# Two slots instead of four in a gather table's rows, and whole-set loads with three buffers in the last stage of a four-layer network

## The reference, cut to what matters

```
layer 0: y = leaky(bn(conv1x1(x)));  xp = inproj(y)
         t = leaky(bn(depthwise3x3(y)));  offset, mask = linear(t), softmax(linear(t))
         for each pixel, 4 groups of 64 channels, 9 points:
             bilinear sample of xp at pixel + dilated tap + offset   (4 corners), times mask, summed
         outproj, bn, squeeze-excite, two-layer MLP, residual
layer 1: grouped 3x3 convolution with kernels rotated by a predicted angle, modulated
layer 2: linear attention (8 heads of 64), 1x1 output, batch norm over all 4 images
layer 3: channels 0-63 kept; 64-127 an 11x1, 128-191 a 1x11, 192-255 a 3x3 grouped
         convolution with weights rounded to 4 bits
```

## Time and profile before

| | us |
|---|---|
| median of 3 runs | 7485.81 (7482.09 to 7492.41) |
| the profiled execution: time | 7487.15 |
| the profiled execution: span | 7485.3 |
| POOL busy | 4751.4 (63%) |
| DVE busy | 5173.2 (69%) |
| PE busy | 3828.6 (51%) |
| ACT busy | 1072.8 (14%) |
| chain that ended last: POOL, its issue gaps, PE | 49%, 22%, 13% |

### The profile page before, as it was taken

How to read it: one execution, slowest core, us unless ns; L and a number is a source line. 1 busy time by engine, 2 the same in 40 slices (tenths; PEclk the granted TensorE clock), 3 DMA queues, 4 the chain that set the end, 5 groups by cost and what they waited for, 6 DMA issues and landing times.

```text
span 7485.3 us, 45646 instructions
## 1 busy us (share of the span) xinstructions
PE 3828.6 (51%) x10560; PEld 2011.8 (27%) x10560; DVE 5173.2 (69%) x5212; ACT 1072.8 (14%) x1619; POOL 4751.4 (63%) x4676
## 2 busy tenths in 40 slices
PE   5243142351475526632764346426656652589957
PEld 3121021220232214411322124213223431234523
DVE  3778778786777768866777679767777975432545
ACT  1110100000111002211110022101001210121333
POOL 0577777777777777777777777777777777200000
PEclk9666576675687767866887678768878876799978
DMA  6373563754433333355333333553333355201067
GB/s 167 109 206 98 178 183 99 220 149 138 148 122 124 101 103 116 123 203 173 122 123 113 103 111 123 191 181 128 122 113 105 122 175 178 79 34 36 34 177 166
DMA packets 681090, 991.26 MB, mean 132 GB/s; under 512 B 413984, under 2 KB 483616, under 8 KB 665248
## 3 DMA queue, kind: packets, MB, share of 16 engines
q0 software_dynamic: 221184, 604.27, 25.2%
q1 hardware_dynamic: 459808, 385.87, 17.2%
HBM read 792.21 MB, written 197.59 MB: 132 GB/s over the span
## 4 chain that ended last, share of the span: by engine, by line
POOL 49%; issue 22%; PE 13%; DVE 9%; DMA 4%; SPq 2%; ACT 1%; DVEq 0%; POOLq 0%; ACTq 0%
POOL ring L369 48%; PE PS L690 12%; DVE ring L1337 3%; DVE dbuf L1343 2%; DMA img<-d_dram 2%; DMA ring<-table,idx_stage 1%; SPq L483 1%; ACT img L1059 1%; DMA cb<-o_dram 1%; DVE sm L1749 0%; DMA o_dram<-img 0%; POOL idx_stage L385 0%; DMA d_dram<-dbuf 0%; SPq L618 0%; SPq L639 0%
## 5 line engine op out<-in xcount | busy, mean ns | idle before, releaser
L369 POOL DMA_INDIRECT ring<-table,idx_stage x4608 | 4720.1, 1024 | 1435.2 <-issue 1370.1
L1343 DVE TENSOR_REDUCE dbuf<-ring 128x64 f32<-128x2304 f32 x512 | 2070.1, 4043 | 45.9 <-DMA d_dram<-dbuf 18.4
L1337 DVE TENSOR_TENSOR ring<-ring,wt 128x576 f32<-128x576 f32 x2048 | 1414.0, 752 | 973.7 <-DMA ring<-table,idx_stage 855.1
L690 PE MATMUL PS<-img,wb_sb 128*128 128x512 f32 (+1 forms) x3328 | 1646.8, 656 | 468.9 <-DVE img L1402 296.4
L690 PE MATMUL PS<-img,wa_sb 128*128 (+1 forms) x1984 | 931.4, 631 | 666.5 <-DVE img L1723 248.3
L690 PEld LDWEIGHTS PS<-img,wb_sb 128*128 128x128 f32 x3328 | 694.9, 213 | 1387.0 <-issue 1098.4
L690 PEld LDWEIGHTS PS<-img,wa_sb 128*128 128x128 f32 x1984 | 398.4, 203 | 1170.1 <-issue 1079.3
L690 PE MATMUL PS<-sm,params 128*128 128x4 f32 (+1 forms) x32 | 9.1, 355 | 863.1 <-DVE sm L1381 762.0
L690 PE MATMUL PS<-wa_sb,cb 128*128 128x108 f32 (+1 forms) x1024 | 238.8, 399 | 371.8 <-DVE cb L1402 371.8
L787 PE MATMUL PS<-params,img 128*128 128x128 f32 x256 | 62.9, 427 | 689.1 <-DMA img<-d_dram 689.1
L1059 ACT ACTIVATE img<-PS,sm 128x512 f32<-128x512 f32 x384 | 247.5, 680 | 1092.9 <-PE PS L690 1092.9
(11 more groups left out here) (191 smaller groups left out, 2977.5 us busy)
## 6 DMA issues: line engine op xcount, KB each, us to landing
ring<-table,idx_stage POOLq DMA_INDIRECT x4608, 2.9
table<-cb SPq DMA_DIRECT2D x128, 512.0 KB, 7.3
img<-y_dram SPq DMA_DIRECT2D x64, 512.0 KB, 6.6
q_dram<-img SPq DMA_DIRECT2D x32, 1024.0 KB, 4.3
img<-q_dram SPq DMA_DIRECT2D x32, 1024.0 KB, 6.9
img<-in_x SPq DMA_DIRECT2D x8, 2048.0 KB, 12.2
y_dram<-cb SPq DMA_DIRECT2D x64, 256.0 KB, 3.0
d_dram<-dbuf SPq DMA_DIRECT2D x128, 128.0 KB
```

What stands on the lines that cost most here:

```text
L369: nc.gpsimd.indirect_dma_start(out=ring[:, g, p * CORNERS * GC:(p + 1) * CORNERS * GC], out_offset=None, in_=tab[b], in_offset=bass.Indire ...
L690: return nc.tensor.matmul(o, l, r, start=start, stop=stop, **kw)
L1337: last = vec.tensor_tensor(rg, rg, weights.unsqueeze(2).to_broadcast([P, n, GC]), ALU.mult)
L1343: vec.tensor_reduce(dbuf[:, j, g * GC:(g + 1) * GC], ring[:, g, :].rearrange("p (k c) -> p c k", c=GC), AX_X, ALU.add).then_inc(sem("ring_ ...
```

## The change

- A table row has two slots, the pixel and the pixel one image row below, 512 B. The groups lie one behind the other (`(g r)`), so that the next row is the pixel to the right, and one gather reads two rows, 1 KB. `xp` is stored twice instead of four times; index and weight order follow.
- The zero rows at the start are 16 transfers from 32 partitions, 32 KB each, instead of 16 from 64 partitions, 256 KB each.
- o and x2 lie in DRAM by set: a set is 128 contiguous rows of 8 KB. L3 loads it in one transfer; L2b stores each chunk's o and x2 in two halves of 64 partitions each.
- o has a third buffer, in `idx`. Sets 0 to 2 of the first image are loaded ahead of L2b of the last image; in L3 `load_o(0, (3,))` stands ahead of `load_x(1)`, and later sets are issued one to three sets earlier.

```diff
-TAB_FRONT = W + 1
-TAB_ROWS = HW + P
+TAB_ROWS = W + HW
+TAB_STORES = 2
+OBUFS = 3
-        tab = [dram(f"table{b}", [G * TAB_ROWS, CORNERS * GC]) for b in range(B)]
+        tab = [dram(f"table{b}", [G * TAB_ROWS, 2 * GC]) for b in range(B)]
-        o_dram = dram("o_dram", [B, P, KC, 2, HALFP])
-        x2_dram = dram("x2_dram", [B, P, KC, 2, HALFP])
+        o_dram = dram("o_dram", [B, SETS, P, HALFP])
+        x2_dram = dram("x2_dram", [B, SETS, P, HALFP])
-        obuf = [cb[:, j * HALFP:(j + 1) * HALFP] for j in range(2)]
+        obuf = [cb[:, j * HALFP:(j + 1) * HALFP] for j in range(2)] \
+            + [idx[:].rearrange("p j n -> p (j n)")[:, 0:HALFP].bitcast(F32)]
...
-                    pieces = [(t, first) for t in tab for first in (0, P // 2, HW, HW + P // 2)]
+                    pieces = [(t, first, slot) for t in tab for slot in range(2) for first in (slot * HW, slot * HW + W // 2)]
...
-                        for j, back in enumerate((0, 1, W, W + 1)):
-                            first = c * (CHUNK * G) + (TAB_FRONT - back) * G
-                            sp.dma_start(tab[b][bass.ds(first, CHUNK * G), :].rearrange("(p q) c -> p q c", q=SUBS * G)
-                                         [:, :, j * GC:(j + 1) * GC], src).then_inc(sem(f"t_stored{h}"), 16)
+                        rows_at = tab[b].rearrange("(g r) c -> r g c", g=G)
+                        for slot in range(2):
+                            sp.dma_start(rows_at[bass.ds(c * CHUNK + (1 - slot) * W, CHUNK)][:, :, slot * GC:(slot + 1) * GC]
+                                         .rearrange("(p s) g c -> p s g c", s=SUBS),
+                                         xpt[h].rearrange("p (s g c) -> p s g c", s=SUBS, g=G)).then_inc(sem(f"t_stored{h}"), 16)
...
                         for store, src in ((x2_dram, i2[6 + h]), (o_dram, i2[4 + h])):
-                            sp.dma_start(store[b].rearrange("p k two n -> p (k two) n")
-                                         [:, :, bass.ds(c * (CHUNK // 2), CHUNK // 2)],
-                                         src.rearrange("p (a n) -> p a n", a=KC * 2)).then_inc(sem(f"o_stored{h}"), 16)
+                            for j in range(2):
+                                sets = store[b].rearrange("(j k) (two c) n -> j c (k two) n", j=2, two=2)[j]
+                                sp.dma_start(sets[:, :, bass.ds(c * (CHUNK // 2), CHUNK // 2)],
+                                             src[j * SC:(j + 1) * SC, :].rearrange("p (a n) -> p a n", a=KC * 2))\
+                                    .then_inc(sem(f"o_stored{h}"), 16)
...
-                    load_o(0, (0, 1))
+                    load_o(0, (0, 1, 2))
...
+            def set_of(store, b, q):
+                return store[b][q % 2 * KC + q // 2]
...
             def load_x(b, sets=range(SETS)):
                 for q in sets:
-                    for par in range(2):
-                        sp.dma_start(x3[b % 2][par * SC:(par + 1) * SC, q * HALFP:(q + 1) * HALFP], rows_of(x2_dram, b, q, par))\
-                            .then_inc(sem(f"e_x{b % 2}{q}"), 16)
+                    sp.dma_start(x3[b % 2][:, q * HALFP:(q + 1) * HALFP], set_of(x2_dram, b, q)).then_inc(sem(f"e_x{b % 2}{q}"), 16)
...
-                    if b * SETS + q >= 2:
-                        sp.wait_ge(sem("eA"), b * SETS + q - 1)
-                    for par in range(2):
-                        sp.dma_start(obuf[q % 2][par * SC:(par + 1) * SC], rows_of(o_dram, b, q, par))\
-                            .then_inc(sem(f"e_o{q % 2}"), 16)
+                    m = b * SETS + q
+                    if m >= OBUFS:
+                        sp.wait_ge(sem("eA"), m - OBUFS + 1)
+                    sp.dma_start(obuf[m % OBUFS], set_of(o_dram, b, q)).then_inc(sem(f"e_o{m % OBUFS}"), 16)
...
+                load_o(0, (3,))
                 load_x(1)
-                load_o(0, (2, 3))
-                if B > 1:
-                    load_o(1, (0, 1))
+                load_o(1, (0, 1, 2))
...
-                        if b + 1 < B and form < 2:
-                            load_o(b + 1, (form + 2,))
+                        if form == 0 and b + 1 < B:
+                            load_o(b + 1, (3,))
+                        if form and b + 2 < B:
+                            load_o(b + 2, (form - 1,))
...
                         if form == 0 and b + 2 < B:
-                            load_o(b + 2, (0, 1))
+                            load_o(b + 2, (2,))
```

More of the change, by code:

```diff
@@ L460, in A @@
                     sp.wait_ge(sem("zeros"), 1)
-                    pieces = [(t, first) for t in tab for first in (0, P // 2, HW, HW + P // 2)]
-                    for (t, first), name in zip(pieces, store_sems + ["pads_stored"] * (len(pieces) - len(store_sems))):
-                        sp.dma_start(t.rearrange("(r g) c -> r g c", g=G)[first:first + P // 2],
-                                     dbuf[0:P // 2, 0, :].unsqueeze(1).to_broadcast([P // 2, G, C])).then_inc(sem(name), 16)
+                    pieces = [(t, first, slot) for t in tab for slot in range(2) for first in (slot * HW, slot * HW + W // 2)]
+                    for (t, first, slot), name in zip(pieces, store_sems + ["pads_stored"] * (len(pieces) - len(store_sems))):
+                        sp.dma_start(t.rearrange("(g r) (s c) -> s r g c", g=G, s=2)[slot][first:first + W // 2],
+                                     dbuf[0:W // 2, 0, 0:GC].unsqueeze(1).to_broadcast([W // 2, G, GC])).then_inc(sem(name), 16)
                     for name in store_sems:
@@ L1251, in lb @@
                         done(act, "bP", n)
-                        act.wait_ge(sem(f"o_stored{h}"), m_ * 32 + 16)
+                        act.wait_ge(sem(f"o_stored{h}"), m_ * 64 + 16)
                         room(act, "bS", n)
@@ L1271, in scaled @@
                     for q in range(SETS):
-                        act.wait_ge(sem(f"e_o{q % 2}"), 32 * (b * 2 + q // 2 + 1))
+                        m = b * SETS + q
+                        act.wait_ge(sem(f"e_o{m % OBUFS}"), 16 * (m // OBUFS + 1))
                         at = q % 2 * KC + q // 2
-                        A_(obuf[q % 2], obuf[q % 2], ACT.Identity, bias=obn4[:, SETS + at:SETS + at + 1], scale=obn4[:, at:at + 1])\
+                        A_(obuf[m % OBUFS], obuf[m % OBUFS], ACT.Identity, bias=obn4[:, SETS + at:SETS + at + 1], scale=obn4[:, at:at + 1])\
                             .then_inc(sem("eB"), 1)
@@ L1546, in A @@
                 made = idx[:, 0, :] if b == 0 else img1[:, 0:TILES * PTS].bitcast(U32)
-                vec.scalar_tensor_tensor(out=tp(made), in0=tp(T(7)), scalar=float(G),
-                                         in1=v("g_base").unsqueeze(1).to_broadcast([P, TILES, PTS]),
-                                         op0=ALU.mult, op1=ALU.add)\
+                vec.tensor_tensor(tp(made), tp(T(7)), v("g_base").unsqueeze(1).to_broadcast([P, TILES, PTS]), ALU.add)\
                     .then_inc(sem("idx_made"), 1)
@@ L1566, in A @@
                 Wt = (wt[:] if b == 0 else img2[:, 0:4608]).rearrange("p (n j) -> p j n", j=CORNERS)
-                for j, (my, wx) in enumerate(((4, 0), (4, 2), (5, 0), (5, 2))):
+                for j, (my, wx) in enumerate(((4, 0), (5, 0), (4, 2), (5, 2))):
                     last = vec.tensor_tensor(Wt[:, j, :], T(my), T(wx), ALU.mult)
@@ L1989, in _lay_out @@
     put("gy_base", hy.reshape(P, -1).astype(f))
-    put("g_base", np.broadcast_to(np.arange(PTS) // K2 + TAB_FRONT * G, (P, PTS)).astype(f))
+    put("g_base", np.broadcast_to(np.arange(PTS) // K2 * TAB_ROWS + W, (P, PTS)).astype(f))
     ow = g(L + "off_w")
```

13 lines of the change are left out of this document (5 added, 8 removed).

## The result

The changed kernel takes 7386.13 us in the median of 4 runs (7378.7 to 7394.4), the kernel before 7483.95 (7478.17 to 7492.41, 4 runs on the same chip): a ratio of 0.9871 [0.9856, 0.9886]. The profiled execution has a span of 7392.6 and a time of 7394.4. The spans differ by 92.7 us. The other 5 us are the spread of executions: this one is 8.3 above its median, the profiled one of before 3.2 above its own.

What follows compares the result with a forecast made beforehand. POOL's own gather pace was taken as the bound from 236 to 6421 us, leaving head, tail and few stalls to shorten. -36.5 - 11.7 + 6 + 8 - 12.8 - 24.5 = -71.5 us gave 7415; range 7396 to 7438.

Steps and rivals of the forecast that it cites:

- table stores' -36.5: Head, stage A1: half of the table's stores go, A1 becomes PE-bound and ends at 104.5 instead of 140.95, -36.5 us.
- zero rows' -11.7: Head: smaller zero transfers free SP's queue by 15, so PE starts at about 28.1 instead of 39.84, -11.7 us.
- Both bounds that were rejected: Head: zero rows gain 0 if issues still cost 1.9 us; table stores gain only -28 if packets keep their number.
- Rival 3: Head: table stores slow down in DRAM; +5 us at a quarter more per piece, 7452 at twice the cost; chance 0.05.
- Gathers: Gather stretch: each gather still takes 1 KB for one index per partition, so thinner traffic gives POOL 0.
- Rival 2: Gather stretch: a gather pays per table row and gets slower; +2180 us at half of the 946 ns; chance 0.04.
- +6 for the last image: L2b of the last image: stores from 64 partitions run at 194 GB/s, so it loses 6 us; bounds +1.2 and +12.
- my lower bound of +1.2: L2b of the last image: only SP's two extra issues cost time, if the half-set stores cost nothing.
- +8 for POOL's stalls: L2b of images 0 and 1: later-landing half-set stores lengthen POOL's stalls by 4 us each, +8 us; bounds 0 and +10.
- Rival 4: L2b: the half-set stores starve the stage at both bounds (+12, +10), giving 7423; chance 0.05.
- -12.8: L3, first image: sets 0 to 2 loaded during L2b let DVE run four sets in a row, -12.8 us.
- -24.5: L3, later images: three buffers and faster loads remove most of DVE's waits, periods about 49 us, -24.5 us.

Runs made afterwards that it cites:

- narrow: Kernel before with the gathers' index no longer counting pixels by four rows, so rows come from a quarter of the table (wrong pixels): 7464.98 us, ratio 0.9984.
- parts9: Changed kernel with DVE's multiply over a gathered unit in 9 instructions instead of 4: 7360.45 us, ratio to before 0.9845.
- sets_only: Kernel before with the set layout, half-set stores, whole-set loads, third buffer and new L3 order, but the old table: 7461.1 us, ratio 0.9963.
- whole_two: Changed kernel with whole-set loads kept, but two buffers for o and the old order of loads in L3: 7406.95 us, ratio to before 0.9907.
- halves_three: Changed kernel with each L3 set loaded in two transfers of 64 partitions, three buffers and new order kept: 7405.46 us, ratio to before 0.9904.
- zeros_both_halves: Kernel before with the 16 zero-row stores reading partitions 0 to 63 and 64 to 127 in turn: 7489.65 us in one execution.
- table_only: Kernel before with the two-slot table and its zero rows alone: 7424.61 us, ratio 0.9909.
- parts12: Changed kernel with DVE's multiply over a unit in 12 instructions instead of 4: 8492.17 us on a slow chip (before 8636.54), ratio 0.9811.
- parts2: Changed kernel with DVE's multiply over a unit in 2 instructions instead of 4: 8609.52 us on a slow chip, ratio to before 0.9981.

## Why the prediction was right and where it was not

The whole came out 26 us faster than forecast and below the range: one term was put at nothing and was not, and one was too dear.

**Head, right.** The table stores' -36.5 and the zero rows' -11.7 make -48.2; the first gather moved by -47.2. Both bounds that were rejected (issues that cost what they cost, stores that keep their number of packets) did not come. Rival 3 neither: stores by four take 7.5 us and A1 no longer waits for them. The zero rows' issues take 1.0 us each, not 0.6, and are through at 20.4, not 15; DVE was ready only at 27.6, so it cost nothing.

**Gathers: the step that failed.** "Each still takes 1 KB for one index per partition ... so the thinner traffic gives POOL nothing: 0." The work of a gather is unchanged and its median too, but the term was read from the median and the traffic alone. The table's part of the stream is -12 to -17 us. narrow shows the cause to be which rows are read, not the stores. That the gain goes through a shorter hold under DVE's multiply rests on the excess under that multiply (5 to 13 us less in each kernel whose rows lie closer), on its growth with the landing time within one trace, and on parts9; no run changed the landing without the rows. The rows to have read were in the groups of before: a mean of 1024 ns beside a median of 946 is 360 us over 4608 gathers, 219 of them under this multiply, an unexamined term with both signs open. Rival 2 looked at a dearer gather only. Its mechanism did not appear.

**Half-set stores: mechanism right, size wrong.** +6 for the last image was +0.9 here (+1.8 in sets_only, +1.1 in parts9; +3.4 in whole_two, which has before's order of loads, and +4.6 in halves_three, with the half loads of o ahead of the stage). The row taken was zeros from one half only at 194 GB/s; the case of alternating halves was in no row, and the value lies at my lower bound of +1.2. The +8 for POOL's stalls is -3 to +8 by the streams, which cannot resolve it, and about +6 by the gaps (79 us in the mean of before, zeros_both_halves, narrow and table_only, 85 in that of after, sets_only, halves_three and whole_two). Rival 4 did not come.

**L3, right.** -12.8 and -24.5 make -37.3 against -36.9. The reason given, load rate and then order, is confirmed as a pair. The periods, the waits of 6.8 us and the 419 GB/s are as listed.

**The sum.** From -71.5 to the spans' -92.7 there are -21.2 us: -16.4 in the stream of the gathers, -5.1 in L2b, -1.1 between them, +1.0 and +0.4 in the head and L3. The range failed because the gathers had no bound below nothing: 10 to 15 us there would have reached to the measured time.

## What to carry to other kernels

Where a mean stands well above its median on the engine that sets the pace, look for the neighbour that holds it, one instruction at a time, before calling its term zero: moving or splitting that neighbour may be worth as much as a part of the edit in hand (here some 19 us for one constant). Split it by measurement: 9 parts shortened the gathers, 12 lengthened them. Price a transfer from a row that has its neighbours in the queue as well as its shape: a half-width store cost a half-width rate alone, and a small part of that between stores of the other half. When two parts of an edit feed one wait, measure each alone, since the second part measured is worth much less than the first.

## What the runs showed of the hardware

- Gathers of 128 rows of 1 KB land about 0.1 us sooner when the rows lie within a quarter of the memory and partly repeat (1.92 against 1.98 to 2.02 us from the issue's end to the first use, and 1.89 to 1.91 with the new table).
- An indirect gather on POOL that starts under a two-input multiply of DVE is held, as a rule until that instruction ends (0.33 us with 0.4 to 0.5 us left, 1.05 us with 1.1 to 1.4 left); under a one-input sum of 4 us it is not held at all. Under a row of 12 short multiplies (a new one every 0.27 us) 28% of the gathers are held until the last of them ends, 1.24 us in the mean; under rows of 2, 4 or 9 it is some 1% or less.
- Stores of 1 KB pieces from alternating partition halves overlap (346 GB/s in zeros_both_halves), while loads of 8 KB rows into alternating halves do not (220 to 223 GB/s in before and halves_three; a piece takes 600 ns there, 309 in the changed kernel). Why they differ was not tried: the piece's size and the direction both differ.
- On two of the chips the kernel before took 15 to 17% longer than elsewhere, and parts12 and parts2 there took about as long as it. Their traces have the head and L3 as long as elsewhere and 1000 to 1500 us of gaps between POOL's gathers. In them ACT stood idle 1440 to 1990 us and DVE 790 to 1450 us in waits for something that the profile can only call another core or an unknown queue; the traces of before, the changed kernel and parts9 have no such wait. No run here shows the cause.
